# ReLU, rounding and transposition of the normalized rows: from PE and PSUM to VectorE and a transposing DMA

## The reference

```python
h = jnp.maximum(_layernorm(x, axis=-1), 0.0)
q = split_heads(h @ Wq.T)
k = split_heads(h @ Wk.T)
v = split_heads(h @ Wv.T)
bias = (adj + adj)[:, None]
a = jnp.einsum('bhnd,bhmd->bhnm', q, k) * scale + bias
row_nonzero = jnp.any(a != 0, axis=-1, keepdims=True)
a = jnp.where(row_nonzero, a, -jnp.inf)
p = jax.nn.softmax(a, axis=-1)
p = jnp.where(jnp.isnan(p), 0.0, p)
o = jnp.einsum('bhnm,bhmd->bhnd', p, v)
o = o.transpose(0, 2, 1, 3).reshape(B, N, D)
x = x + o @ Wo.T
```

## Time and profile before

| | us |
|---|---|
| median of 3 runs | 1005.82 |
| the runs | 1005.83, 1004.63, 1005.82 |
| the profiled execution | 1005.16 |
| its span, from the first to the last instruction | 1003.4 |

### The profile page before, as it was taken

The page is one execution under the profiler, slowest core; times in us unless marked ns, Lnnn a source line. Parts: engine busy times, 40 slices in busy tenths (PEclk is TensorE's granted clock), DMA queues, the critical chain, the costliest instruction groups (busy, mean ns, idle before and its releaser), DMA issues.

```text
span 1003.4 us, 33752 instructions
## 1 busy us (share of the span) xinstructions
PE 959.6 (96%) x11580; PEld 660.2 (66%) x11580; DVE 850.0 (85%) x3092; ACT 934.5 (93%) x3049; POOL 862.3 (86%) x936
## 2 busy tenths in 40 slices
PE   5879999999999999999999999999999999999965
PEld 4656776666677666777666677766666776667632
DVE  6778998888989888898988889988889898888863
ACT  5799999999999999999999999999999999999992
POOL 2278998989998898999888899989889988889894
PEclk9989999999999999999999999999999999999979
DMA  6289999999999999999999999999999999999995
GB/s 251 49 148 195 183 190 194 183 193 186 190 191 184 195 178 187 194 199 180 192 177 198 183 203 184 189 194 178 198 183 197 186 191 193 177 185 176 175 175 119
DMA packets 573818, 183.62 MB, mean 183 GB/s; under 512 B 547024, under 2 KB 555216, under 8 KB 573648
## 3 DMA queue, kind: packets, MB, share of 16 engines
q1 hardware_dynamic: 573648, 181.48, 100.9%
HBM read 29.36 MB, written 16.78 MB: 46 GB/s over the span
## 4 chain that ended last, share of the span: by engine, by line
PE 56%; DVE 28%; issue 8%; ACT 5%; POOL 1%; DMA 1%; DVEq 0%; POOLq 0%; ACTq 0%; SPq 0%
PE ps L1045 35%; DVE logits L752 15%; PE ps L1113 9%; PE ps L1063 7%; DVE stats L649 4%; ACT probs L547 3%; PE ps L942 3%; DVE q_lo L815 2%; DVE o_norm L782 2%; PE ps L1089 1%; DVE some L770 1%; ACT p L560 1%; PE ps L1019 1%; DMA w_nat<-in_L_gnn_Wq 1%; DVE row_min L752 1%
## 5 line engine op out<-in xcount | busy, mean ns | idle before, releaser
L430 POOL TENSOR_TENSOR p<-probs,p 128x512 f16<-128x512 f32 x512 | 586.4, 1161 | 89.9 <-ACT p L560 89.7
L547 ACT ACTIVATE probs<-logits,row_min 128x256 f32<-128x256 f32 x1024 | 513.6, 511 | 3.8 <-DVE row_min L752 3.8
L752 DVE CUSTOM_DVE_ANT_0 logits<-ps,adj_s,sigma 128x256 f32<-128x256 f32 x1024 | 438.0, 475 | 7.1 <-PE ps L1063 7.0
L560 ACT ACTIVATE p<-probs 128x512 f16<-128x512 f32 x512 | 323.5, 632 | 0.0
L1045 PE MATMUL ps<-ht_hi,w_hi 128*128 128x256 f16 x1024 | 280.2, 274 | 7.7 <-DVE q_lo L815 2.6
L1045 PE MATMUL ps<-ht_lo,w_hi 128*128 128x256 f16 x1024 | 279.4, 273 | 0.0
L1045 PE MATMUL ps<-ht_hi,w_lo 128*128 128x256 f16 x1024 | 279.4, 273 | 0.0
L547 ACT ACTIVATION_READ_ACCUMULATOR probs<-logits,row_min 128x1 f32 x1024 | 209.8, 205 | 0.0
L1045 PE MATMUL ps<-wo,o_hi 128*128 128x512 f16 x496 | 149.2, 383 | 3.8 <-POOL o_lo L456 3.8
L1045 PEld LDWEIGHTS ps<-ht_hi,w_hi 128*128 128x128 f16 x1024 | 100.1, 98 | 36.1 <-DVE q_lo L815 13.0
L1045 PEld LDWEIGHTS ps<-ht_lo,w_hi 128*128 128x128 f16 x1024 | 100.4, 98 | 14.0
(11 more groups left out here) (90 smaller groups left out, 1571.0 us busy)
## 6 DMA issues: line engine op xcount, KB each, us to landing
xs<-in_x SPq DMA_DIRECT2D x32, 512.0 KB, 4.6
out<-xs SPq DMA_DIRECT2D x64, 256.0 KB, 2.9
adj_raw<-in_adj SPq DMA_DIRECT2D x32, 256.0 KB, 3.2
pt<-p SPq DMA_TRANSPOSE x256, 4.0
w_nat<-p SPq DMA_TRANSPOSE x256, 3.4
w_nat<-in_L_gnn_Wq SPq DMA_DIRECT2D x2, 512.0 KB, 5.4
w_nat<-in_L_gnn_Wk SPq DMA_DIRECT2D x1, 1024.0 KB, 8.3
w_nat<-in_L_gnn_Wv SPq DMA_DIRECT2D x1, 1024.0 KB, 11.3
```

What stands on the lines that cost most here:

```text
L430: g.tensor_tensor(p16[:, c % 2, k, 1], probs[:, h % 4].rearrange("p u n -> p (u n)"), p16[:, c % 2, k, 0], ALU.subtract).then_inc(p_split, 1)
L547: e = a.activation(probs[:, h % 4, u, :], logits[:, h % 4, u, :], ACT.Exp, bias=row_min[:, t.par(d), u, h:h + 1], scale=-1.0, accum_out=ro ...
L560: a.activation(p16[:, c % 2, k, 0], probs[:, h % 4].rearrange("p u n -> p (u n)"), ACT.Copy)\
L752: v.tensor_tensor_reduce(out=logits[:, h % 4, u, :], in0=ps[:, S_BANK + h % HC, N * u:N * u + N], in1=adj_s[:, t.par(d), u, :], scale=sigm ...
```

## The change

For batches from 3 on (H_TURNED) PE no longer turns xn. POOL makes xn as before. At steps 6 and 10 of DVE's list, where the two take_h stood, a new function rest_of_h works on one row block u each: a tensor_scalar writes max(xn, 0) as f16 into the first half of h16[:, u], and a scalar_tensor_tensor writes max(xn, 0) minus that into the second half; between them it waits on its own semaphore h_hi_dve. All operands are in SBUF, where xn lies with the rows in partitions. h16 is block 2 of w16. At step 11 SP waits for both (h_split) and issues one transposing DMA of 128 partitions by 2048 f16 columns into ht, which now holds hi and lo of both row blocks in one tensor, [P, 2, NU, 2 * NC, P]. PE's step 0 waits for its landing (ht_in). ACT does nothing for these batches (H_BY_ACT is empty, so round_h isn't called). POOL waits for h_split of the batch before, ahead of the new rstd. Batches 0 to 2 are turned by PE as before, by row block instead of by column block, into the new layout. The projections read ht in two runs of 128 columns.

```diff
+H_TURNED = 3
+H_BY_ACT = ()
+H_HI_STEPS, H_LO_STEPS = (5, 5), (6, 10)
...
+        h16 = w16[:, 2]
...
-        ht_hi = sb("ht_hi", [P, 2, NC, N], F16)
-        ht_lo = sb("ht_lo", [P, 2, NC, N], F16)
+        ht = sb("ht", [P, 2, NU, 2 * NC, P], F16)
...
+        def h_rows_free(eng, b):
+
+            if b == H_TURNED:
+                eng.wait_ge(wo16_in, 16 * NC)
+            else:
+                eng.wait_ge(ht_in, 16 * (b - H_TURNED))
...
+                    if s == 11 and later(t, 2) and h_by_dma(t.batch(2)):
+                        b = t.batch(2)
+                        sp.wait_ge(h_split, NU * (b - H_TURNED + 1))
+
+                        sp.wait_ge(pj_full, NJ * t.batch(0) + 6)
+                        sp.dma_start_transpose(ht[:, b % 2].rearrange("p u l n -> p (u l) n"),
+                                               h16[:, 0:NU].rearrange("p u n -> p (u n)")).then_inc(ht_in, 16)
...
+                if h_by_dma(b - 1):
+
+                    pool.wait_ge(h_split, NU * (b - H_TURNED))
...
+            def rest_of_h(b, u):
+
+                n = b - H_TURNED
+                if u in H_BY_ACT:
+                    dve.wait_ge(h_hi_act, len(H_BY_ACT) * n + H_BY_ACT.index(u) + 1)
+                else:
+                    dve.wait_ge(xn_ready, NU * b + u + 1)
+                    h_rows_free(dve, b)
+                    v.tensor_scalar(h16[:, u, 0:D], xn[:, u, :], 0.0, None, ALU.max).then_inc(h_hi_dve, 1)
+                    dve.wait_ge(h_hi_dve, (NU - len(H_BY_ACT)) * n + u - len(H_BY_ACT) + 1)
+                v.scalar_tensor_tensor(out=h16[:, u, D:2 * D], in0=xn[:, u, :], scalar=0.0,
+                                       in1=h16[:, u, 0:D], op0=ALU.max, op1=ALU.subtract).then_inc(h_split, 1)
...
-                for c in range(2):
-                    for u in range(NU):
-                        m = tr(ps[:, bank, N * c + P * u:N * c + P * u + P],
-                               xn[:, u, P * (2 * k + c):P * (2 * k + c) + P], ident[:])
+                for c in range(NC):
+                    m = tr(ps[:, bank, P * c:P * c + P], xn[:, k, P * c:P * c + P], ident[:])
...
-                                        HT[b][:, t.par(1), kc, :], i == 0, i == len(steps) - 1))
+                                        ht[:, t.par(1), :, NC * b + kc, :], i == 0, i == len(steps) - 1))
...
+                    if j == 0 and h_by_dma(t.batch(1)):
+
+                        pe.wait_ge(ht_in, 16 * (t.batch(1) - H_TURNED + 1))
```

More of the change, by code:

```diff
@@ L173, in emit @@
         ln_stats = sem("ln_stats")
+        h_hi_act = sem("h_hi_act")
+        h_hi_dve = sem("h_hi_dve")
+        h_split = sem("h_split")
+        ht_in = sem("ht_in")
         rstd_ready = sem("rstd_ready")
@@ L230, in emit @@
             for at, key in sorted(slot_uses):
+                if key[0] == "h" and h_by_dma(key[1]):
+                    continue
                 if 0 <= key[1] < NB and not (key[0] == "y" and key[2] not in Y_C):
@@ L304, in h_turns, with h_parts @@
             at = (10, 13) if t.first else (5, 8)
-            return [k for k in range(2) if at[k] == s and later(t, 2)]
+            return [k for k in range(2) if at[k] == s and later(t, 2) and not h_by_dma(t.batch(2))]
         def h_rests(t, s):
             at = (10, 13) if t.first else (6, 10)
-            return [k for k in range(2) if at[k] == s and later(t, 2)]
+            return [k for k in range(2) if at[k] == s and later(t, 2) and not h_by_dma(t.batch(2))]
+        def h_parts(t, s, steps):
+            return [u for u in range(NU) if steps[u] == s and later(t, 2) and h_by_dma(t.batch(2))]
+        def h_rows_free(eng, b):
[3 more added lines that the diff above has]
+                eng.wait_ge(ht_in, 16 * (b - H_TURNED))
         first = Slot(0, -1, False, False, True)
@@ L401, in layernorm @@
             def layernorm(t, d):
-                pool.wait_ge(ln_stats, NU * (t.batch(d) + 1))
+                b = t.batch(d)
+                pool.wait_ge(ln_stats, NU * (b + 1))
+                if h_by_dma(b - 1):
+                    pool.wait_ge(h_split, NU * (b - H_TURNED))
                 g.tensor_tensor(rstd[:], var_s[:], minus_half[:], ALU.pow).then_inc(rstd_ready, 1)
-                pool.wait_ge(rstd_ready, t.batch(d) + 1)
-                if d == 2:
-                    pool.wait_ge(aux_full, aux_after("h", t.batch(1), 1))
+                pool.wait_ge(rstd_ready, b + 1)
+                if d == 2 and not h_by_dma(b - 1):
+                    pool.wait_ge(aux_full, aux_after("h", b - 1, 1))
                 for u in range(NU):
-                    g.tensor_scalar(xn[:, u, :], xs[:, t.batch(d) % X_RING, u, :], neg_mean[:, u:u + 1],
+                    g.tensor_scalar(xn[:, u, :], xs[:, b % X_RING, u, :], neg_mean[:, u:u + 1],
                                     rstd[:, u:u + 1], ALU.add, ALU.mult).then_inc(xn_ready, 1)
@@ L524, in take_h, with round_h @@
                 act.wait_ge(aux_full, aux_after("h", b, k))
-                a.activation(ht_hi[:, b % 2, 2 * k:2 * k + 2, :],
-                             ps[:, bank, :].rearrange("p (c n) -> p c n", c=2), ACT.Relu)\
+                a.activation(ht[:, b % 2, k, 0:NC, :].rearrange("p c n -> p (c n)"), ps[:, bank, :], ACT.Relu)\
                  .then_inc(aux_hi, 1)
+            def round_h(b, u):
+                act.wait_ge(xn_ready, NU * b + u + 1)
+                h_rows_free(act, b)
+                a.activation(h16[:, u, 0:D], xn[:, u, :], ACT.Relu).then_inc(h_hi_act, 1)
             take_h(0, 0)
@@ L630, in slot @@
                         take_h(t.batch(2), k)
+                    for u in h_parts(t, s, H_HI_STEPS):
+                        if u in H_BY_ACT:
+                            round_h(t.batch(2), u)
             run(act, slot)
@@ L656, in ln_mean_var @@
                 dve.wait_ge(stat_step, step + 2 * NU)
+                need(dve, xn_ready, NU * t.batch(d))
                 v.tensor_scalar(neg_mean[:], mean_var[:, :, 0], -1.0, None, ALU.mult).then_inc(ln_stats, 1)
@@ L722, in take_h @@
                 dve.wait_ge(aux_hi, 2 * b + (k + 1))
[L723 to L725 removed]
+                v.scalar_tensor_tensor(out=ht[:, b % 2, k, NC:2 * NC, :].rearrange("p c n -> p (c n)"),
+                                       in0=ps[:, bank, :], scalar=0.0,
+                                       in1=ht[:, b % 2, k, 0:NC, :].rearrange("p c n -> p (c n)"),
                                        op0=ALU.max, op1=ALU.subtract).then_inc(aux_taken, 1)
+            def rest_of_h(b, u):
+                n = b - H_TURNED
+                if u in H_BY_ACT:
+                    dve.wait_ge(h_hi_act, len(H_BY_ACT) * n + H_BY_ACT.index(u) + 1)
[6 more added lines that the diff above has]
+                                       in1=h16[:, u, 0:D], op0=ALU.max, op1=ALU.subtract).then_inc(h_split, 1)
             for u in range(NU):
@@ L862, in slot @@
                             take_h(t.batch(2), k)
+                        for u in h_parts(t, s, H_LO_STEPS):
+                            rest_of_h(t.batch(2), u)
                     for b, u in residuals(t, s):
```

10 lines of the change are left out of this document (4 added, 6 removed).

## The result

The changed kernel takes 1070.99 us in the median of 4 runs (1070.32 to 1071.29); the kernel before, run beside it, 1005.23 (1004.48 to 1005.83). The ratio is 1.0654, 95% interval 1.0635 to 1.0672. The forecast was 1020 with a range up to 1042: the sign was right, the size was not. The profiled execution had a span of 1069.3 us.

A forecast was written before the change was run, and what follows sets the result against it. No engine full; the order of waits, a PE half then a DVE half, bounds the 29.5 us batch. PE's 1.03 us gain is outweighed by DVE's blocks waiting for POOL: +0.5 us times 29, 1005.2 + 14.5 = 1019.7, said 1020; range 984 to 1042.

The forecast's parts named there:

- 28.5 us a batch for equal work: PE's turns, 1.03 us on the path, go; with only equal work in their place, 29.5 falls to 28.5 us.
- up to 0.8 us a batch: At PE's first product: loss to the transposing DMA's landing if DVE were not delayed, up to 0.8 us a batch.
- The prices: DVE's new blocks, steps 6 and 10: tensor_scalar 0.35, semaphore 0.1, subtraction 0.55 us, plus two POOL waits of 0 to 1.16.
- the forecast's sum: DVE's cross-check for a batch: 26.7 us of work, 2.6 of block waits, 0.9 at two L770: 30.2 us.
- two L770 behind the blocks: DVE's small instruction L770 after each new block meets POOL and waits, 0.9 us in all for two.
- The walk through the PE half: Steps 4 to 12: blocks cost +1.4 and +1.8 us, PE stalls at scores of steps 8 and 12; middle +0.5 a batch.
- The DVE half left as it was: Steps 13 to 3 (logits, residuals, statistics, q_lo) start 0.73 us later in the walk; no growth of their own was counted.
- room that added work eats: DVE's waits in the PE half for k_hi (2.04 us) and v_hi (1.25), about 3.3 a batch, taken as spare time.
- The rival of a favourable phase: DVE's blocks meet POOL well; scores of step 8 stall 0.8, 0.2 us a batch gained: 999 us, chance 0.14.
- the walk with POOL 0.5 us earlier: Same walk, POOL earlier against DVE: waits 0.14 and 0.6 at step 6, DVE half starts 0.33 us later.
- The heavier case: DVE's blocks: four waits of a whole L430, tensor_scalar 0.60: 6.0 us less 3.3 idle, +2.7, 1084 us; chance 0.10 above 1042.
- What would show it: Signs: tensor_scalar 0.3 to 1.5 us, subtractions 0.6 to 1.7, k_hi and v_hi waits gone, PE awaiting row_min, period near 30.

The follow-up runs named there:

- e6: Changed kernel without both new DVE instructions and without the transposing DMA of h, PE multiplying what lies in ht: 978.50 us, ratio 0.9731.
- e1: Changed kernel without both new DVE instructions (h16 keeps what it held, DVE only signals), the transposing DMA kept: 1028.72 us, ratio 1.0233.
- e7: Changed kernel with both new DVE instructions but without the transposing DMA of h: 1071.69 us, ratio 1.0661.
- e4: Changed kernel with POOL's long subtraction L465 split into two instructions of one row block each: 1043.03 us, ratio 1.0396.
- e10: Kernel before with DVE's subtraction L724 (input from PSUM) done twice for batches 3 to 31: 1008.64 us, ratio 1.0040.
- e11: Kernel before with DVE's subtraction L724 (input from PSUM) done three times for batches 3 to 31: 1042.11 us, ratio 1.0369.
- e2: Changed kernel with ACT writing relu of the normalised x into PSUM, DVE rounding and subtracting from there, POOL making only rstd and shift: 1038.13 us, ratio 1.0328.
- e13 to e15: Kernel before, kernel before with L724 three times, changed kernel, each without some and with neg_mean, var_s by single elements: 994.28, 1026.29, 1032.77 us.
- e8: Kernel before with neg_mean and var_s each as two instructions of one element a partition: 999.84 us, ratio 0.9947.
- e12: Changed kernel without both new DVE instructions, the transposing DMA of h issued at SP's step 7 instead of 11: 1039.32 us, ratio 1.0350.

## Why the prediction was wrong

**What bounds the kernel, and PE's gain.** The forecast was right that PE's turns lay on the path: without anything in their place the kernel takes 978.5 us (e6). But 28.5 us a batch for equal work was out of reach with the DMA where it is: its issue and landing bound the period at 30.3 us (e1). The forecast's loss of "up to 0.8 us a batch" there was 1.8 (30.3 - 28.5), 1.54 of it PE's wait at the first product. It cost the prediction nothing only because DVE was later still (e7), which the forecast had said.

**The prices.** These were right, nearly to the number. All 58 subtractions took 1520, 1536 and 1569 ns (minimum, median, maximum), which is what was left of a POOL instruction plus 0.53 to 0.56 us; the forecast had 0.55. The tensor_scalar ends 0.27 to 0.30 us past POOL's end, where the estimate was 0.35, bounds 0.16 to 0.60. Block 1 cost 1.79 us more than before (forecast 1.4), block 2 cost 1.53 more (2.13 from 539.38 to 541.51, forecast 1.8): together 3.32 against 3.2. DVE's busy time in a batch went from 25.86 to 30.06, +4.2, and the forecast's sum has +4.3 (30.2). That this sum agrees is luck: 0.9 of it was to be waits of two L770 behind the blocks, and L770 took no more in the PE half than before (0.63 us against 0.65), while 1.14 us came in the DVE half, where the forecast has nothing. (The Trainium skill, SBUF — State Buffer, section SBUF: two separate sides, calls the shared port pair an exclusive lock that the first to start gets for its whole instruction. By that rule, the trace agrees: the wait lasts to the end of POOL's instruction, and e4 makes it 0.51 us shorter by making that shorter.)

**The walk through the PE half.** Its times were right: its end came 0.36 us a batch later; the forecast said 0.73 or 0.33 by phase and took 0.5. Its path was not. The forecast has PE stall at the scores of steps 8 and 12, which wait for DVE's logits. In the trace PE stalls earlier, ahead of its projections, 1.05 us for k_lo and 0.92 us for v_lo (the two PE rows above), and the scores follow without a stall of that kind. That both ways lead to nearly the same time is luck.

**The DVE half left as it was: the step that failed.** The walk ends where the DVE half starts, at "+0.73 us a batch", and the 0.5 us of the sum is that shift alone. The forecast counted DVE's 2.04 us of waiting for k_hi and 1.25 for v_hi as room that added work eats, and put the growth of the DVE half at nothing, without a reason. That half grew by 1.98 us of the 2.34 that a batch lost. The rows of DVE in that half, after:

```profile
545.75 0.48 DVE L810 CUSTOM_DVE_ANT_0 logits<-ps,adj_s,sigma 128x256 f32<-128x256 f32 x1 [0.20 <-PE ps L1125]
547.28 0.69 DVE L840 TENSOR_TENSOR o_norm<-ps,w_nat 128x512 f32<-128x512 f32 x1 [0.23 <-issue]
552.12 0.79 DVE L895 TENSOR_SCALAR some_qk<-some_qk 128x32 f32<-128x32 f32 x1
557.37 0.85 DVE L702 TENSOR_SCALAR neg_mean<-mean_var 128x2 f32<-128x2 f32 x1
```

1. 0.84 us is new idle time. It is the 0.23 ahead of o_norm and the 0.61 ahead of the residual (shown above): DVE waits for PE (ahead of o_norm the row names no releaser, but PE's values, which o_norm reads, end at 547.14; in the kernel before they end at 543.72, 0.86 us ahead of o_norm). Before, PE ran ahead of DVE; now k_lo and v_lo, delayed by the blocks in front of them, hold PE's projections (39.5 and 33.6 us of waits), so scores, values and the output projection come just when DVE wants them or after. So DVE's waiting in the PE half wasn't all free: in e10 and e11 about 1.2 us of it could be filled with plain work, not 3.3.
2. 0.94 us of the 1.14 of added busy time is in small old instructions that met POOL at a worse moment: some_qk 0.79 instead of 0.21, neg_mean 0.85 instead of 0.57, some 0.49 instead of 0.41. In every steady batch neg_mean starts 0.33 us into an instruction of POOL where it was 0.6, and some_qk 0.4 us where it was 0.99. 0.2 us is spread over the rest.

**The forecast's phases.** The rival of a favourable phase and the walk with POOL 0.5 us earlier were judged in the PE half alone. The runs say that the phase counts for the small instructions of the DVE half as much: single elements for two of them moved the changed kernel by 34 us, and the kernel before by 5; and in e2, whose new instructions never wait, some_qk alone takes 0.84 us a batch more than in the kernel before.

**Rivals.** The heavier case had the right side with the wrong mechanism: it asked for a whole L430 at four waits. What happened had about the forecast's waits and a room for them of about a third of the size. With that room, the forecast's own numbers would have given: 3.2 us of added block time less 1.2 of room, less nothing for PE's turns (with PE waiting, its gain is idle time), +2.0 us a batch, or 1063 us. That is worked out after the fact and not shown: it leaves out the small instructions, the room was measured with PE's turns still there, and the sum is 8 us short.

**What would show it.** Seen as said: tensor_scalar of 0.61 to 0.92 us (its lowest and highest), long subtractions, k_hi no longer waited for, PE not waiting for the DMA. Said and hardly seen: PE waiting for row_min ahead of the scores (17.6 us in the whole kernel, 11.5 before). Not said: PE ahead of its projections waiting for k_lo, v_lo and q_lo.

**What stays open.** How the changed kernel's own 1.98 us divide between PE's lateness and the small waits is read from its rows; e13 to e15 support it, but taking the small waits away also moved the new ones. That a small instruction's wait goes by the moment at which it meets POOL is in the rows. Why it comes at just that moment in each kernel is not shown, and with it stays open why neg_mean and var_s by single elements brought 34 us, when DVE's busy time fell by 29.6: no run held the phase still.

## What to carry to other kernels

In this kernel an engine's waiting was free room only as far as nothing that it makes behind the wait was wanted at once. Before counting on such room, look up who waits for the instruction after the wait (here PE, for the bank that v_lo frees), and take the room from a run with plain work added there; that is one kernel, and here it would have shown that the room is less than half of what was counted. Where two engines exclude each other for whole instructions, price a new instruction at its length plus the rest of the other's, and expect every old instruction of that kind to change its wait. An operand in PSUM, or a single element a partition, stays out of it.

## What the runs showed of the hardware that I had not expected

- A tensor_scalar of 1 element a partition took 0.141 to 0.156 us (e8, 128 of them) whatever POOL did; one of 2 elements takes 0.15 when it comes between POOL's instructions (L703) and 0.85 in the median, 1.0 at most, when it meets one (L702). Two of one element cost less than one of two that waits. (The Trainium skill, VectorE: DVE Perf Modes, section What auto-detection actually checks, wants for the mode with both ports an outermost non-unit dimension that is even or equal in source and destination. A single element has no such dimension; by that rule, the trace agrees.)
- A recorded start that is earlier by little doesn't mean being first. The tensor_scalar whose recorded start lay 0.01 us before that of POOL's L488 waited to its end.
- The wait goes both ways: POOL's subtraction behind a held DVE instruction took 1.58 us instead of 1.16.
- The tensor_scalar of 512 f32 elements ends 0.28 us after it is let in, about half of the subtraction's 0.53 to 0.56. The estimate in the forecast rested on that factor of two, and the trace now has it.
- The transposing DMA of 128 partitions by 2048 f16 columns held SP's queue for 1.49 to 4.56 us and landed after 4.3 to 6.9 (1.56 to 2.94 and 4.4 to 6.4 in the changed kernel). In e12 the transposes of p behind it were so late that PE waited 33.9 us for them.
